# A fused two-layer graph kernel: in its second graph stage the logits joined with the turning, the second normalisation on ScalarE, the neighbour weightings one round later

## The chip, the cores and the metric
The kernel runs on one core of one Trainium2 chip. Its whole computation is one launch. The metric is the device time of that launch in microseconds, a median over runs.

## What is computed
The input is `x` (64 graphs of 256 nodes with 256 features, fp32) and a 0/1 adjacency `adj` (64 x 256 x 256). Two layers follow, each a graph part and a feed-forward part with a residual and a layer normalisation. Layer 0's feed-forward part is an LSTM over the nodes of each graph with a gate, and layer 1's graph part is a normalised graph convolution. The changed stage does the end of the first and all of the second, and the normalisation after it:

```python
lstm_out = _lstm(x, W_ih, W_hh, b_ih, b_hh)
logits = jnp.einsum('bth,lh->btl', lstm_out, W_lin) + b_lin
g = argmax(logits, axis=-1)[..., None]
w = g * lstm_out
inc = jnp.cumsum(w, axis=1)
prefix = inc - w
suffix = inc[:, -1:, :] - inc
x2 = x1 + 2.0 * lstm_out + prefix * fw_att + suffix * bw_att
...
adj = adj + eye(n)
deg_inv_sqrt = adj.sum(axis=-1) ** -0.5
adj_norm = deg_inv_sqrt[:, :, None] * adj * deg_inv_sqrt[:, None, :]
x3 = x2 + adj_norm @ (layernorm(x2) @ W) + b
xn3 = layernorm(x3)
```

`x3` and `xn3` are then used by layer 1's feed-forward part.

## The kernel before
The kernel has five stages, one after the other, with a barrier of blocks between them: the first graph stage, the LSTM, the second graph stage (`stage_gnn1`, L1022), the tropical stage, and the last feed-forward stage. The change touches the second graph stage alone. In the trace it lies between 1552 and about 2156 us.

A graph is a tile of 256 nodes by 256 features, held as 128 partitions by two blocks; `t` counts blocks of nodes (NT = 2) and `k` blocks of features (KD = 2). The work on the graphs is a software pipeline. The helper `rounds` gives every engine the same sequence of rounds, `r` = 0 to 67. In round `r` a section written `if live(lag)` works on graph `r - lag`; the first 8 and the last 6 rounds are written out, those between are a loop of two. Inside a round each engine has its own fixed order of sections, and semaphores join the engines. Semaphore values count graphs: `wait_past(act, wh_ready, n)` waits until `n` graphs have been weighted. The order of each engine in a full round is this (the lag in brackets):

- TensorE: cumulative products `y` from the weightings (2, L1300 to L1305), turning of `x3` (4), products with `W` into `ps_w` (3, L1319), logits (0, L1330) and turning of `h_t` into `ps_h` (0, helper `turn`, L1291), aggregation with `adjt` (3, L1341), turning of `xn3` (4), turning of `xn` (2).
- VectorE: `x2` from `y` and `s` (2, L1391), its statistics (L1369, L1375), `x2b` (L1396), normalisation `xn3` (4, L1380), normalisation `xn` (2, also L1380), logits with bias and `picked` (0, L1413, L1415), four weightings into `whf` and `whb` (0, L1421), `x3` (3, L1433) and its statistics, `is_zero` and `deg_safe` (2), `s` = `x1` + `h2` (0, L1452).
- ScalarE: copy of `x3t` (4), `hs` from `ps_w` scaled by `dinv` (3, L1250), `h2` = 2 `ps_h` (0, L1258), the state of the next graph gathered into `h_t` (-1, L1235), row sums of `adj` (2, L1267), copy of `xn3t` (4), copy of `xn_t` (2).
- GpSimd: `vare` and `rstd` from the statistics of `x2` (2, L1202, L1204), the identity added to `adjt` (2, L1209), `vare3` and `rstd3` (3, L1215, L1217), then `power`, `keep` and `dinv` (2, to L1226).
- SyncE issues the stores of `x3t`, `xn3` and `xn3t` and the loads of `adjt`, `adj` and `x1`, in that mixed order, each behind a wait.

`h2`, `x2`, `x3`, `xn`, `h_t` and each PSUM tile have one buffer; `s`, `whf`, `whb`, `x2b`, the loaded tiles and the three outputs have two. Before the first round TensorE and VectorE wait until all constants have landed (`CONST_DMAS`, 11 of them). In rows of the trace the stage's prefix and the digits are left out of names: `g_x` stands for x1, x2 and x3, `g_xn` for xn and xn3, `g_rstd` for rstd and rstd3, `g_h` for h2, `g_ht` for h_t.

Of the kernel before, what the change touches and what calls it, by code (L numbers as in the profile page):

```python
# [1021 lines left out]
def stage_gnn1(nc, a, hx, x1_dram, x3t_dram, xn3t_dram, xn3_dram):  # L1022
# [3 lines left out]
    with ExitStack() as ctx:  # L1026
# [6 lines left out]
        def sem(name):  # L1033
# [4 lines left out]
        w_lin = sb("g1_wlin", [P, KD, 2])  # L1038
        b_lin = sb("g1_blin", [P, NT, 2])
# [14 lines left out]
        h2 = sb("g1_h2", [P, NT, D])  # L1054
        logit = sb("g1_logit", [P, NT, 2])
# [21 lines left out]
        one = sb("g1_one", [P, NT])  # L1077
# [6 lines left out]
        ps_logit = ps("g1_ps_logit", [P, NT, 2])  # L1084
        ps_h = ps("g1_ps_h", [P, NT, D])
# [13 lines left out]
        h_t_ready, h_done, h2_ready, logit_ready, picked_ready, wh_ready, y_done = (  # L1099
            sem("g1_" + n) for n in ("h_t_ready", "h_done", "h2_ready", "logit_ready", "picked_ready", "wh_ready",  # L1100
# [10 lines left out]
            sem("g1_" + n) for n in ("x3_ready", "stats3_ready", "mv3_ready", "vare3_ready", "rstd3_ready", "xn3_ready"))  # L1111
        x3t_done, x3t_ready, xn3t_done, xn3t_ready = (
            sem("g1_" + n) for n in ("x3t_done", "x3t_ready", "xn3t_done", "xn3t_ready"))
        CONST_DMAS = 11
# [22 lines left out]
        def _(sp):  # L1137
            sp.dma_start(w_lin[:, :, :], a["w_lin_t"].rearrange("(k p) c -> p k c", p=P)).then_inc(const_in, 16)
# [51 lines left out]
        def _(pool):  # L1190
# [3 lines left out]
            pool.wait_ge(consts_set, 3)  # L1194
            pool.wait_ge(const_in, 16 * CONST_DMAS)

            def body(graph, live):
# [33 lines left out]
        def _(act):  # L1231
# [6 lines left out]
            def body(graph, live):  # L1238
# [13 lines left out]
                if live(0):  # L1252
                    n, i, j = graph(0)

                    act.wait_ge(h_done, n + 1)
                    wait_past(act, wh_ready, n)
                    wait_past(act, s_ready, n)
                    act.activation(h2[:, :, :], ps_h[:, :, :], ACT.Copy, scale=2.0).then_inc(h2_ready, 1)  # L1258
# [25 lines left out]
        def _(pe):  # L1284
# [9 lines left out]
            def body(graph, live):  # L1294
# [27 lines left out]
                if live(0):  # L1322
# [37 lines left out]
        def _(dve):  # L1360
            dve.memset(ones_sq[:, :], 1.0).then_inc(ones_set, 1)
            dve.wait_ge(const_in, 16 * CONST_DMAS)
            dve.tensor_scalar(fw[:, :], fw[:, :], 0.5, None, ALU.mult)
# [20 lines left out]
            def body(graph, live):  # L1384
# [1563 lines left out]
```

## Time and profile before

| what | value |
|---|---|
| median of 3 runs | 6029.61 us (6028.96 to 6030.96) |
| the profiled execution | 6013.3 us, its span 6011.5 us |
| TensorE busy | 5471.9 us, 91% |
| VectorE busy | 4967.6 us, 83% |
| ScalarE busy | 3371.2 us, 56% |
| GpSimd busy | 1711.0 us, 28% |
| mean granted TensorE clock | 0.965 |

Busy time is summed per engine, and the engines run beside each other. TensorE's matmul records are pipelined and overlap, so that a busy share near 100% is not the same as work at full rate; the start times of its records tell more. One fp32 product leaves two records in the trace, one turn of a 128x128 block a single one.

### The profile page before, as it was taken

The page shows a single profiled execution, that of the slowest core. Times are in us where ns is not written, and L with a number is a line of the kernel's source. Part 1 is how long each engine was busy: PE and PEld are TensorE (multiplying, and loading weights), DVE is VectorE, ACT ScalarE, POOL GpSimd, SP SyncE. Part 2 cuts the span into 40 slices and gives each one's busy share as a digit, 9 for nine tenths or more (in the row PEclk, how much of TensorE's full clock was granted, in tenths as well). Part 3 has the DMA queues.
Part 4 walks back from the last instruction along what each step waited for, and adds up shares of the span by engine and source line. Part 5 has one row for each costly group of instructions (what it writes and reads, how often), then busy time and mean ns, then how long its engine had stood idle before and what let it go on. Part 6 is the DMA issues. An engine that isn't in the chain of part 4 may idle for free. (4 is left out here: it accounts for less than half of the span.)

```text
span 6011.5 us, 111926 instructions
## 1 busy us (share of the span) xinstructions
PE 5471.9 (91%) x33194; PEld 3624.3 (60%) x33194; DVE 4967.6 (83%) x9615; ACT 3371.2 (56%) x6793; POOL 1711.0 (28%) x3552
## 2 busy tenths in 40 slices
PE   9998999999899969999999985875759999999999
PEld 6666888888788856666666653443434444444444
DVE  8996664444699969999999997986859999999998
ACT  6664444444455546666666651221228787877787
POOL 3331000000255536666666651375530000000000
PEclk9999999999899989999999997987979999999999
DMA  4442001000355522222222211365541212222221
GB/s 136 135 135 69 0 11 50 0 0 0 96 176 176 177 90 73 73 73 73 73 73 72 71 67 32 114 219 179 171 161 66 89 63 85 69 84 83 71 84 49
DMA packets 359806, 529.10 MB, mean 88 GB/s; under 512 B 28256, under 2 KB 298208, under 8 KB 359680
## 3 DMA queue, kind: packets, MB, share of 16 engines
q1 hardware_dynamic: 323376, 401.62, 20.5%
q0 software_dynamic: 36304, 126.13, 6.1%
q8 instruction: 38, 0.62, 0.0%
q14 instruction: 88, 0.72, 0.0%
HBM read 298.52 MB, written 229.14 MB: 88 GB/s over the span
## 5 line engine op out<-in xcount | busy, mean ns | idle before, releaser
L1894 PE MATMUL t_fetched<-t_wpart,t_onehot 128*128 128x512 f32 x4096 | 1222.0, 420 | 35.8 <-DVE t_tout L1999 15.9
L1999 DVE SCALAR_TENSOR_TENSOR t_tout<-t_fetched,t_top,t_tout 128x1024 f32<-128x1024 f32 x896 | 1149.0, 1282 | 36.3 <-PE t_fetched L1894 4.8
L1894 PEld LDWEIGHTS t_fetched<-t_wpart,t_onehot 128*128 128x128 f32 x4096 | 691.8, 188 | 269.2 <-DVE t_tout L1999 131.2
L2832 DVE SCALAR_TENSOR_TENSOR f_line<-f_hinge,f_vec,f_line 128x1024 f32<-128x1024 f32 x512 | 655.2, 1280 | 82.5 <-ACT f_hinge L2710 48.3
L2322 PE MATMUL ts_fetched<-t_wpart,ts_onehot 128*128 128x512 f32 x1608 | 508.7, 451 | 165.2 <-ACT ts_onehot L2297 65.3
L961 PE MATMUL l_ps<-l_wih,l_x 128*64 128x128 f32 (+1 forms) x6144 | 531.6, 308 | 1.0 <-DVE l_ps L597 1.0
L2322 PEld LDWEIGHTS ts_fetched<-t_wpart,ts_onehot 128*128 128x128 f32 x1608 | 305.6, 208 | 316.6 <-DVE ts_tout L2390 202.3
L961 PE MATMUL l_ps<-l_whh,l_ht 128*64 128x128 f32 (+1 forms) x6144 | 492.6, 309 | 0.0
L2762 PE MATMUL f_pso<-f_fused,f_wd 128*128 128x512 f32 x1024 | 461.9, 594 | 23.1 <-DVE f_ox L2828 23.1
L2749 PE MATMUL f_psc<-f_x,f_wc 128*128 128x512 f32 x1024 | 482.8, 594 | 0.0
L925 ACT ACTIVATE l_act<-l_ps 128x128 f32<-128x128 f32 x1024 | 253.9, 276 | 407.0 <-PE l_ps L961 407.0
L2749 PE MATMUL f_psg<-f_x,f_wg 128*128 128x512 f32 x1024 | 481.2, 592 | 0.0
L2294 ACT ACTIVATE ts_dist<-ts_index,t_pminus 128x256 f32<-128x256 f32 (+2 forms) x140 | 79.5, 568 | 653.6 <-PE ts_index L2313 544.5
L961 PEld LDWEIGHTS l_ps<-l_wih,l_x 128*64 128x64 f32 x6144 | 388.7, 137 | 75.4 <-issue 1.8
L2710 ACT ACTIVATE f_hinge<-f_pst,f_vec 128x1024 f32<-128x1024 f32 x384 | 430.8, 1122 | 0.0
L961 PEld LDWEIGHTS l_ps<-l_whh,l_ht 128*64 128x64 f32 x6144 | 372.5, 137 | 80.9 <-DVE l_ht L617 0.2
L2390 DVE SCALAR_TENSOR_TENSOR ts_tout<-ts_fetched,ts_top,ts_tout 128x1024 f32<-128x1024 f32 x296 | 380.0, 1284 | 14.0 <-PE ts_fetched L2322 3.5
L2762 PEld LDWEIGHTS f_pso<-f_fused,f_wd 128*128 128x128 f32 x1024 | 193.2, 190 | 273.5 <-issue 230.6
L2749 PEld LDWEIGHTS f_psg<-f_x,f_wg 128*128 128x128 f32 x1024 | 194.6, 190 | 245.1 <-issue 245.1
L2832 DVE SCALAR_TENSOR_TENSOR f_line<-f_spare,f_vec,f_line 128x1024 f32<-128x1024 f32 x224 | 287.8, 1285 | 44.3 <-DVE f_line L2832 44.3
L1842 ACT ACTIVATE t_tout<-t_fetched,t_top 128x1024 f32<-128x1024 f32 x128 | 142.9, 1117 | 322.8 <-PE t_fetched L1894 322.8
L2719 ACT ACTIVATE f_spare<-f_pst,f_vec 128x1024 f32 x224 | 241.2, 1138 | 137.2 <-DVE f_pause L2857 136.8
(384 smaller groups left out, 10720.8 us busy)
## 6 DMA issues: line engine op xcount, KB each, us to landing
t<-t_tout SPq DMA_DIRECT2D x128, 512.0 KB, 2.6
f_t<-t SPq DMA_DIRECT2D x64, 1024.0 KB, 5.3
g_adj<-in_adj SPq DMA_DIRECT2D x128, 256.0 KB, 3.0
g_adjt<-in_adjt SPq DMA_DIRECT2D x128, 256.0 KB, 2.7
t_x<-x_normalised SPq DMA_DIRECT2D x130, 128.0 KB, 2.3
g_x<-in_x SPq DMA_DIRECT2D x64, 256.0 KB, 2.8
x_kept<-g_x SPq DMA_DIRECT2D x64, 256.0 KB, 2.1
g_x<-x_kept SPq DMA_DIRECT2D x64, 256.0 KB, 2.8
```

Of the source, the lines that this page charges most:

```text
L925: act.activation(act_g[q][:, :], gate(j, q), function).then_inc(act_ready[q], 1)
L961: mm = pe.matmul(out[:, :, 0:P] if n > 1 else ps_g[j][c2 * HB:(c2 + 1) * HB, q * LANE:q * LANE + P], source[:, k, :], w[:, k, q:q + n, c2, ...
L1842: act.activation(t_out[j][:, :], fetched[0][:, :], ACT.Identity, bias=top[j][:, 0, 0:1]).then_inc(first_ready, 1)
L1894: mm = pe.matmul(fetched[c % RING][:, h * CH:(h + 1) * CH], one_hot[g][:, c % GRP * P:(c % GRP + 1) * P], w_part[part][:, k, h * CH:(h + 1 ...
L1999: dve.scalar_tensor_tensor(t_out[j][:, :], column[:, :], value, t_out[j][:, :], ALU.add, ALU.max)\
L2322: mm = pe.matmul(fetched[buf][:, h * CH:(h + 1) * CH], one_hot[b][:, at * P:(at + 1) * P], w_part[part][:, half, h * CH:(h + 1) * CH], sta ...
L2390: dve.scalar_tensor_tensor(t_out[j][:, :], column[:, :], top[j][:, c:c + 1], (t_out if c else t_in)[j][:, :], ALU.add, ALU.max).then_inc(f ...
L2710: act.activation(hinge[v][:, k, :], ps_t[:, :], ACT.Relu, bias=column(u, "knot", k))\
L2719: act.activation(spare[:, ds(k, 1), :].rearrange("p o t -> p (o t)"), ps_t[:, :], ACT.Relu, bias=column(u, "knot", k + SURE))
L2749: mm = pe.matmul(ps_[:, :], w_[:, k, u * P:(u + 1) * P], x[j][:, k, h * HB:(h + 1) * HB], start=(k == 0), stop=(k == KD - 1))
L2762: mm = pe.matmul(ps_o[k][:, h * HB:(h + 1) * HB], w_d[:, u, k * P:(k + 1) * P], fused[u % 2][:, h * HB:(h + 1) * HB], start=(u == 0), stop ...
L2832: dve.scalar_tensor_tensor(acc[:, :], source, column(u, "bend", k), acc[:, :], ALU.mult, ALU.add)\
```

## The change
In TensorE's part, the separate logit products and the turning of `h_t` become one product per block: `h_t` is the stationary operand and `turn_lin`, the identity with the two columns of `W_lin` beside it (130 columns), is the moving one. `ps_h` therefore gets a layout of its own with two banks, and holds one pair of partial logits for each `k`. `h2` copies turned state and logits together, 520 columns instead of 512. VectorE adds the two partial logits and twice the bias from `h2` (two small additions instead of one) and picks. This and the weightings move from lag 0 to lag 1 and, within the round, from behind `xn` to behind `x2b`. The second normalisation moves from VectorE to ScalarE, two operations of 128x256 (`Identity` with a scale and a bias per row) behind the copy of `h2`; for it GpSimd computes `minus_mean3` and `shift3` in addition. `s` now waits for `h2` itself. Two more constants are loaded.

```diff
-            sp.dma_start(w_lin[:, :, :], a["w_lin_t"].rearrange("(k p) c -> p k c", p=P)).then_inc(const_in, 16)
+            sp.dma_start(turn_lin[:, :, P:P + 2], a["w_lin_t"].rearrange("(k p) c -> p k c", p=P)).then_inc(const_in, 16)
+            for k in range(KD):
+                sp.dma_start(turn_lin[:, k, 0:P], a["ident"]).then_inc(const_in, 16)
...
                     pool.wait_ge(mv3_ready, n + 1)
+                    wait_past(pool, xn3_ready, n)
+                    pool.tensor_tensor(minus_mean3[:, :], mv3[:, :, 0], minus_one[:, :], ALU.mult)
                     pool.tensor_tensor(vare3[:, :], mv3[:, :, 1], eps[:, :], ALU.add).then_inc(vare3_ready, 1)
                     pool.wait_ge(vare3_ready, n + 1)
                     pool.tensor_tensor(rstd3[:, :], vare3[:, :], half[:, :], ALU.pow).then_inc(rstd3_ready, 1)
+                    pool.wait_ge(rstd3_ready, n + 1)
+                    pool.tensor_tensor(shift3[:, :], minus_mean3[:, :], rstd3[:, :], ALU.mult).then_inc(shift3_ready, 1)
...
                     act.wait_ge(h_done, n + 1)
                     wait_past(act, wh_ready, n)
                     wait_past(act, s_ready, n)
-                    act.activation(h2[:, :, :], ps_h[:, :, :], ACT.Copy, scale=2.0).then_inc(h2_ready, 1)
+                    act.activation(h2[:, :, :, :], ps_h[:, :, :, 0:P + 2], ACT.Copy, scale=2.0).then_inc(h2_ready, 1)
+                if live(4):
+                    n, i, j = graph(4)
+
+                    act.wait_ge(shift3_ready, n + 1)
+                    wait_past(act, x3t_stored[j], 48 * i)
+                    for t in range(NT):
+                        last = act.activation(xn3_out[j][:, t, :], x3[:, t, :], ACT.Identity, scale=rstd3[:, t:t + 1],
+                                              bias=shift3[:, t:t + 1])
+                    last.then_inc(xn3_ready, 1)
                 if live(-1):
                     turned_h(graph(-1)[0])
...
                     pe.wait_ge(h_t_ready, n + 1)
                     wait_past(pe, h2_ready, n)
-                    wait_past(pe, logit_ready, n)
                     for t in range(NT):
                         for k in range(KD):
-                            pe.matmul(ps_logit[:, t, :], h_t[:, k, t * P:(t + 1) * P], w_lin[:, k, :],
-                                      start=(k == 0), stop=(k == KD - 1))
-                    turn(ps_h, h_t).then_inc(h_done, 1)
+                            last = pe.matmul(ps_h[:, t, k, 0:P + 2], h_t[:, k, t * P:(t + 1) * P], turn_lin[:, k, :],
+                                             start=True, stop=True)
+                    last.then_inc(h_done, 1)
...
                     dve.tensor_tensor(x2b[j][:, :, :], x2[:, :, :], b_all[:, :, :], ALU.add).then_inc(x2b_ready, 1)
-                if live(4):
-                    n, i, j = graph(4)
-
-                    dve.wait_ge(rstd3_ready, n + 1)
-                    wait_past(dve, x3t_stored[j], 48 * i)
-                    normalised(n, xn3_out[j], x3, mv3, rstd3, xn3_ready)
+                if live(1):
+                    n, i, j = graph(1)
+
+                    dve.wait_ge(h2_ready, n + 1)
+                    dve.tensor_tensor(half_logit[:, :, :], h2[:, :, 0, P:P + 2], two_b[:, :, :], ALU.add)\
+                       .then_inc(half_logit_ready, 1)
+                    dve.wait_ge(half_logit_ready, n + 1)
+                    dve.tensor_tensor(logit[:, :, :], h2[:, :, 1, P:P + 2], half_logit[:, :, :], ALU.add).then_inc(logit_ready, 1)
+                    dve.wait_ge(logit_ready, n + 1)
+                    dve.tensor_tensor(picked[:, :], logit[:, :, 1], logit[:, :, 0], ALU.is_gt).then_inc(picked_ready, 1)
+                    dve.wait_ge(picked_ready, n + 1)
+                    wait_past(dve, y_done, n - 1)
+                    for wh, att in ((whf, fw), (whb, bw)):
+                        for t in range(NT):
+                            last = dve.scalar_tensor_tensor(wh[j][:, t, :].rearrange("p (k u) -> p k u", k=KD), h2[:, t, :, 0:P],
+                                                            picked[:, t:t + 1], att[:, :].rearrange("p (k u) -> p k u", k=KD),
+                                                            ALU.mult, ALU.mult)
+                    last.then_inc(wh_ready, 1)
                 if live(2):
                     n, i, j = graph(2)
 
                     dve.wait_ge(rstd_ready, n + 1)
                     wait_past(dve, xt_done, n)
                     normalised(n, xn, x2, mv, rstd, xn_ready)
-                if live(0):
-                    n, i, j = graph(0)
-
-                    dve.wait_ge(h_done, n + 1)
-                    dve.tensor_tensor(logit[:, :, :], ps_logit[:, :, :], b_lin[:, :, :], ALU.add).then_inc(logit_ready, 1)
...
-                    dve.wait_ge(h2_ready, n + 1)
-                    wait_past(dve, y_done, n - 1)
-                    for wh, att in ((whf, fw), (whb, bw)):
...
                 if live(0):
                     n, i, j = graph(0)
 
+                    dve.wait_ge(h2_ready, n + 1)
                     dve.wait_ge(x1_loaded[j], 16 * i + 16)
                     wait_past(dve, x2_ready, n - 1)
-                    dve.tensor_tensor(s[j][:, :, :], x1_in[j][:, :, :], h2[:, :, :], ALU.add).then_inc(s_ready, 1)
+                    dve.tensor_tensor(s[j][:, :, :].rearrange("p t (k u) -> p t k u", k=KD),
+                                       x1_in[j][:, :, :].rearrange("p t (k u) -> p t k u", k=KD), h2[:, :, :, 0:P], ALU.add).then_inc(s_ready, 1)
```

## Rows read from the trace of the kernel before

**Rows 1.** Windows: us, busy us by engine (x instructions), PEclk, DMA share, GB/s.
```profile
1800.00:1900.00 100.00, 99.59 (x586) 87.96 (x585) 94.23 (x304) 54.36 (x123) 51.17 (x104) 1.00 0.56 175
```
**Rows 2.** Waits, 1600 to 2129 us: who, for whom, us in total, times, longest.
```profile
DVE g_xn L1380 <- POOL g_rstd L1204: 15.3, 59, 0.3
PEld g_ps_agg L1341 <- ACT g_hs L1250: 14.8, 59, 0.3
```
**Rows 3.** Timeline of VectorE (start us, length us): x2 in rounds 4 and 64.
```profile
1594.81 0.68 DVE L1391 TENSOR_TENSOR g_x<-g_ps_y,g_s 128x512 f32<-128x512 f32 x1
...
2129.93 0.68 DVE L1391 TENSOR_TENSOR g_x<-g_ps_y,g_s 128x512 f32<-128x512 f32 x1
```
**Rows 4.** Timeline of TensorE, one steady round: logits and the turn of h.
```profile
1854.59 0.95 PE L1330 MATMUL g_ps_logit<-g_wlin,g_ht 128*128 128x2 f32 x8
...
1855.40 0.63 PE L1291 MATMUL g_ps_h<-g_ident,g_ht 128*128 128x128 f32 x4
```
**Rows 5.** Timeline of TensorE, same round: turn of xn3, last products of y.
```profile
1857.72 0.58 PEld L1291 LDWEIGHTS g_ps_xn3t<-g_ident,g_xn 128*128 128x128 f32 x4
...
1857.93 0.60 PE L1291 MATMUL g_ps_xn3t<-g_ident,g_xn 128*128 128x128 f32 x4
...
1860.97 0.59 PE L1305 MATMUL g_ps_y<-g_whb,g_after 128*128 128x256 f32 x2
```
**Rows 6.** Timeline of VectorE, same round.
```profile
1853.45 0.68 DVE L1391 TENSOR_TENSOR g_x<-g_ps_y,g_s 128x512 f32<-128x512 f32 x1
...
1855.70 0.73 DVE L1380 TENSOR_SCALAR g_xn<-g_x,g_mv,g_rstd 128x256 f32<-128x256 f32 x2
...
1856.68 1.00 DVE L1380 TENSOR_SCALAR g_xn<-g_x,g_mv,g_rstd 128x256 f32<-128x256 f32 x2 [0.26 <-POOL g_rstd L1204]
...
1857.61 0.15 DVE L1413 TENSOR_TENSOR g_logit<-g_ps_logit,g_blin 128x4 f32<-128x4 f32 x1
...
1857.98 0.88 DVE L1421 SCALAR_TENSOR_TENSOR g_whf<-g_h,g_picked,g_fw 128x256 f32<-128x256 f32 x2
...
1858.78 0.88 DVE L1421 SCALAR_TENSOR_TENSOR g_whb<-g_h,g_picked,g_bw 128x256 f32<-128x256 f32 x2
...
1859.57 0.87 DVE L1433 SCALAR_TENSOR_TENSOR g_x<-g_ps_agg,g_dinv,g_x2b 128x256 f32<-128x256 f32 x2
...
1862.34 0.69 DVE L1391 TENSOR_TENSOR g_x<-g_ps_y,g_s 128x512 f32<-128x512 f32 x1
```
**Rows 7.** Timeline, a late round: hs on ScalarE and the aggregation's weight loads.
```profile
2147.37 0.84 ACT L1250 ACTIVATE g_hs<-g_ps_w,g_dinv 128x256 f32<-128x256 f32 x2 [1.91 <-POOL g_dinv L1226]
2148.26 0.73 PEld L1341 LDWEIGHTS g_ps_agg<-g_hs,g_adjt 128*128 128x128 f32 x4 [1.86 <-ACT g_hs L1250]
```
**Rows 8.** Timeline of ScalarE, steady round: h2, h_t, first of the adj copies.
```profile
1856.07 0.60 ACT L1258 ACTIVATE g_h<-g_ps_h 128x512 f32<-128x512 f32 x1
...
1856.57 1.09 ACT L1235 ACTIVATE g_ht<-hx 128x512 f32 x1
...
1857.57 0.40 ACT L1267 ACTIVATE g_adj<-g_adj 128x256 f32<-128x256 f32 x1
```
**Rows 9.** Timeline of GpSimd, steady round.
```profile
1856.61 0.92 POOL L1209 TENSOR_TENSOR g_adjt<-g_adjt,g_ident 128x128 f32<-128x128 f32 x2
...
1861.60 0.20 POOL L1215 TENSOR_TENSOR g_vare<-g_mv,g_eps 128x2 f32<-128x2 f32 x1 [4.07 <-DVE g_mv L1375]
...
1863.85 0.20 POOL L1226 TENSOR_TENSOR g_dinv<-g_power,g_keep 128x2 f32<-128x2 f32 x1
```
**Rows 10.** Timeline, start of the stage: a constant's issue, the first logits.
```profile
1553.24 0.46 SPq L1139 DMA_DIRECT2D g_ident<-in_ident  x1
...
1563.86 1.87 PE L1330 MATMUL g_ps_logit<-g_wlin,g_ht 128*128 128x2 f32 x8 [14.69 <-DMA g_w<-in_W]
```
**Rows 11.** Windows, a stretch of the tropical stage.
```profile
3750.00:3800.00 50.00, 41.28 (x171) 24.62 (x168) 47.60 (x66) 11.45 (x18) 12.52 (x26) 1.00 0.22 78
```
**Rows 12.** Groups of ScalarE's instructions by line: one of four table loads.
```profile
L1588 ACT ACT_TABLE_LOAD x1 | 1.3, 1283 | 2.8 <-DVE t_scale L1643 2.8
```

More of the change, by code:

```diff
@@ L1037, in stage_gnn1 @@
         w = sb("g1_w", [P, KD, D])
-        w_lin = sb("g1_wlin", [P, KD, 2])
-        b_lin = sb("g1_blin", [P, NT, 2])
+        turn_lin = sb("g1_turnlin", [P, KD, P + 2])
+        b_lin, two_b = sb("g1_blin", [P, NT, 2]), sb("g1_twob", [P, NT, 2])
         ones_sq = sb("g1_ones_sq", [P, P])
@@ L1053, in stage_gnn1 @@
         h_t = sb("g1_ht", [P, KD, N])
-        h2 = sb("g1_h2", [P, NT, D])
-        logit = sb("g1_logit", [P, NT, 2])
+        h2 = sb("g1_h2", [P, NT, KD, P + 2])
+        half_logit, logit = sb("g1_halflogit", [P, NT, 2]), sb("g1_logit", [P, NT, 2])
         picked = sb("g1_picked", [P, NT])
@@ L1076, in stage_gnn1 @@
         eps = sb("g1_eps", [P, NT])
-        one = sb("g1_one", [P, NT])
+        one, minus_one = sb("g1_one", [P, NT]), sb("g1_minusone", [P, NT])
+        minus_mean3, shift3 = sb("g1_minusmean3", [P, NT]), sb("g1_shift3", [P, NT])
         row_sum = sb("g1_row_sum", [P, NT])
@@ L1083, in stage_gnn1 @@
         dinv = [sb(f"g1_dinv{j}", [P, NT]) for j in range(2)]
-        ps_logit = ps("g1_ps_logit", [P, NT, 2])
-        ps_h = ps("g1_ps_h", [P, NT, D])
+        ps_h = ps("g1_ps_h", [P, NT, KD, 2 * P])
         ps_y = ps("g1_ps_y", [P, NT, D])
@@ L1098, in stage_gnn1 @@
         x3t_stored = [sem(f"g1_x3t_stored{j}") for j in range(2)]
-        h_t_ready, h_done, h2_ready, logit_ready, picked_ready, wh_ready, y_done = (
-            sem("g1_" + n) for n in ("h_t_ready", "h_done", "h2_ready", "logit_ready", "picked_ready", "wh_ready",
+        h_t_ready, h_done, h2_ready, half_logit_ready, logit_ready, picked_ready, wh_ready, y_done = (
+            sem("g1_" + n) for n in ("h_t_ready", "h_done", "h2_ready", "half_logit_ready", "logit_ready", "picked_ready", "wh_ready",
                                      "y_done"))
@@ L1111, in stage_gnn1 @@
             sem("g1_" + n) for n in ("x3_ready", "stats3_ready", "mv3_ready", "vare3_ready", "rstd3_ready", "xn3_ready"))
+        shift3_ready = sem("g1_shift3_ready")
         x3t_done, x3t_ready, xn3t_done, xn3t_ready = (
             sem("g1_" + n) for n in ("x3t_done", "x3t_ready", "xn3t_done", "xn3t_ready"))
-        CONST_DMAS = 11
+        CONST_DMAS = 13
         LAST = 4
@@ L1193, in _ @@
             pool.memset(one[:, :], 1.0).then_inc(consts_set, 1)
-            pool.wait_ge(consts_set, 3)
+            pool.memset(minus_one[:, :], -1.0).then_inc(consts_set, 1)
+            pool.wait_ge(consts_set, 4)
             pool.wait_ge(const_in, 16 * CONST_DMAS)
@@ L1362, in _ @@
             dve.wait_ge(const_in, 16 * CONST_DMAS)
+            dve.tensor_scalar(two_b[:, :, :], b_lin[:, :, :], 2.0, None, ALU.mult)
             dve.tensor_scalar(fw[:, :], fw[:, :], 0.5, None, ALU.mult)
@@ L1408, in body @@
                     normalised(n, xn, x2, mv, rstd, xn_ready)
-                if live(0):
-                    n, i, j = graph(0)
-                    dve.wait_ge(h_done, n + 1)
-                    dve.tensor_tensor(logit[:, :, :], ps_logit[:, :, :], b_lin[:, :, :], ALU.add).then_inc(logit_ready, 1)
-                    dve.wait_ge(logit_ready, n + 1)
-                    dve.tensor_tensor(picked[:, :], logit[:, :, 1], logit[:, :, 0], ALU.is_gt).then_inc(picked_ready, 1)
-                    dve.wait_ge(picked_ready, n + 1)
-                    dve.wait_ge(h2_ready, n + 1)
-                    wait_past(dve, y_done, n - 1)
-                    for wh, att in ((whf, fw), (whb, bw)):
-                        for t in range(NT):
-                            last = dve.scalar_tensor_tensor(wh[j][:, t, :], h2[:, t, :], picked[:, t:t + 1], att[:, :],
-                                                            ALU.mult, ALU.mult)
-                    last.then_inc(wh_ready, 1)
                 if live(3):
```

## The prediction

> **What bounds the stage now.** The change touches one stage, the second graph stage. I read the windows first, to see how full each engine is; then who waited for whom, for what ends the idle time; then one steady round in order of time, because a stage in which three engines are nearly full is set by a loop of waits and not by a share. In the 100 us window TensorE is busy 99.6 us and VectorE 94.2, ScalarE and GpSimd about half [rows 1]. The waits in 59 rounds are small: VectorE waited 15.3 us for GpSimd's `rstd`, TensorE's weight loads 14.8 us for `hs` [rows 2]. VectorE waits for nothing else, and GpSimd's `rstd` comes from VectorE's own statistics, so VectorE with that short trip closes the loop that sets the round. From the start of `x2` in round 4 to its start in round 64 there are 60 rounds: 2129.93 - 1594.81 = 535.1 us, 8.92 us each [rows 3]. TensorE's own work is 8.92 less 14.8/59 = 0.25 of waiting, 8.67 us: almost level, but behind.
>
> **TensorE's part.** From the first turn of `xn3` at 1857.93 to the last pair of `y` at 1860.97 lie 8 turn records of 128 columns and 10 of `y` of 256, in 3.04 us [rows 5]; if the pitch goes by columns that is 28 times 0.109, so a turn takes 0.109 and a record of `y` 0.217. The logits start at 1854.59 and the turning of `h` at 1855.40, 0.81 us, and its four turns are 0.44 [rows 4]: 1.25 us go. In come 4 products of 130 columns, two records each: 8 x 0.11 = 0.87 us. TensorE saves 0.38 and has 8.29 us of work. The bounds are the pitch of the logits' records, 0.81 for eight, and that of 256 columns, 1.74, which would be 0.5 worse than today. It lies between `w` products and aggregation, and, as the loop below shows, in TensorE's slack, so I price it at nothing; the cover is over 1 us.
>
> **VectorE's part.** Out goes the second normalisation, 0.73 us (at 1855.70 in [rows 6]). In comes one small addition; `logit` to the first weighting is 1857.98 - 1857.61 = 0.37 for two such operations, so three are 0.55. The four weightings have the same shape; their source now has gaps, priced at nothing for lack of a row. The wait of 0.26 for `rstd` goes, since the weightings now cover it. VectorE's own work falls to about 8.92 - 0.26 - 0.73 + 0.18 = 8.11 us. What counts is the order: the weightings (of the graph before) now stand directly behind `x2b`, ahead of `xn` and `x3`.
>
> **ScalarE's part, and the new loop.** `h2` has one buffer. Its copy already waits for `wh_ready`; that used to mean weightings of the round before and now means those of this round. Behind the copy, in ScalarE's queue, stands the second normalisation. TensorE turns its result before it turns `xn` and before it starts `y` of the next round, and VectorE's `x2` waits for `y`. So one loop goes once round all three engines in every round, from the end of the weightings to the end of the next:
> - a hand-over from engine to engine: 0.05, as from `hs` (2147.37 + 0.84) to the aggregation at 2148.26 [rows 7]; there are three, 0.15.
> - copy of `h2`: the next operation starts 1856.57 - 1856.07 = 0.50 later [rows 8]. (520 columns instead of 512 add 0.01.)
> - second normalisation: two operations of 128x256 with a per-row scale, as `hs`: 0.84 [rows 7].
> - TensorE, turn of `xn3`, turn of `xn`, six products of `y`: from 1857.93 to 1860.97 + 0.59 = 1861.56, 3.63, and 0.07 for the first weight load after an idle gap (between nothing and the 0.21 from load at 1857.72 to product): 3.70 [rows 5].
> - `x2`, statistics, `x2b`: 1855.70 - 1853.45 = 2.25 [rows 6].
> - three small operations, 0.55; weightings 1857.98 to 1858.78 + 0.88 = 1859.66, 1.68 [rows 6]: 2.23.
> Sum: 0.15 + 0.50 + 0.84 + 3.70 + 2.25 + 2.23 = **9.67 us** a round, against 8.92. It binds in the rounds that have both an `h2` and an `xn3`, 4 to 63, which closes 60 intervals: 60 x 9.67 - 535.1 = 45 us more.
>
> Is everything else ready in time? Count from the end of the weightings. ScalarE releases `xn3` at 1.39; `xn` (1.00 at most) is done before that. `y` ends at 5.15. VectorE could be at `x2` by 1.44 + 2.77 = 4.21 (start of `x3` to the next `x2`, 1862.34 - 1859.57 in [rows 6]), so it stands idle for 1 us. TensorE goes on with the turn of `x3`, 0.44, and the `w` products, 8 x 0.217: 7.3. GpSimd's `dinv`: today from `vare3` at 1861.60 to 1863.85 + 0.20 it takes 2.45 [rows 9]; the two new small operations (`minus_mean3` ahead, `shift3` behind the power) add some 0.27 each, so about 3.0; starting near 3.4 (`x3` from 1.44, and 1861.60 - 1859.57 = 2.03 more) it ends near 6.4, before the `w` products. `hs` ends near 8.2, the aggregation near 10.05, and `xn3` of the next round comes at 9.67 + 1.39 = 11.06. So TensorE waits about 1.0 us there each round and its saving is lost in that wait. SyncE's loads of `adjt`, `adj` and `x1` now stand behind a later store of `xn3`; they are issued one to two rounds (10 to 19 us) ahead of their use and cost nothing.
>
> **Unknown costs.** GpSimd's addition to `adjt` (0.92) now falls beside the weightings instead of `xn`. Beside it, `xn` takes 1.00 instead of the 0.73 of `xn3` [rows 6, 9], so another operation might lose up to 0.27; I take nothing, because `x2` at 1862.34 with GpSimd at work beside it takes 0.69 and no row but `xn` shows a loss, and keep 0.27, 16 us, for the range. The Trainium skill (SBUF — State Buffer, Who interferes with whom) says that a VectorE instruction with two SBUF inputs contends with a GpSimd instruction that reads SBUF, which is the case of the weightings beside this addition; by it the sum would be nearer 9.9 us a round, and 61 us in all. Hand-overs: 0 to 0.10 each, -9 to +9 us. The normalisation reads SBUF and not PSUM; the `adj` copy of that shape takes 0.40 [rows 8], a little under half of the 0.84, so down to -4 us.
> Outside the steady rounds: two more constant loads at 0.46 of issue each [rows 10], +1; the first two logit-and-turn groups run before TensorE's clock has risen, 1.87 for the logits' records against 0.95 later [rows 4, 10], and there the joined ones take about twice 0.87 instead of 1.87 and twice 0.44, -2; in rounds 2 and 3 `xn` waits for the weightings, +1 to +2; at the end `shift3` and a slightly longer normalisation, +1. Together +2, between -3 and +5.
>
> The profiled execution took 6013.3 us (span 6011.5), 16 below the median of the three runs; 45 + 2 = 47 gives 6060 on its scale and 6029.6 + 47 = **6077 us** on that of the median. About 0.2%, 12 us, is what a measurement of this kernel can tell from no change.
>
> **Rivals.**
> *Other loops set the round (faster).* If `y` were done before VectorE gets to `x2`, the round would go by VectorE's `x3`, which waits for `xn3` to leave its single buffer: 0.05 + 1.34 + 0.05 + 2.77 + 2.25 + 2.23 = 8.69 us, 14 us less, so 6018. For it: VectorE and TensorE both lose work. Against: from the weightings' end to `y`'s end there are 5.15 us where 4.4 would be break-even, and every piece of them has a row. Chance 0.08, nearly all for a wait that I misread.
> *Gains and losses cancel*: 0.04.
> *The loop, and contention or clock on top (more than 6095).* Weightings with the full 0.27, hand-overs at 0.10: 10.1 us, 6102. TensorE's granted clock is 1.00 here; busy 8.29 of 9.67, 86%, it could fall. A stretch of the tropical stage at 83% busy has 1.00 [rows 11], which speaks against it. At a mean of 0.9 the 3.70 would be 4.1, +25 us. Chance 0.15.
> *A table load before each Identity.* ScalarE's load is 1.28 us [rows 12], one on the loop each round would be +77, 6154. The tropical stage alternates Identity at L1842 and Copy at L1836 without loads between; 0.02.
> *The loop as summed*: 0.71. It ends on the slow side, as do the last two. Faster 0.08, same 0.04, slower 0.88. The range, 6052 to 6104, takes in the loop with all its bounds and leaves out the first, the second and the fourth rival.
>
> **What would show it.** In the after profile: steady rounds of 9.67; VectorE waits some 0.95 us a round in `x2` for `y`, a new first row in its waits; TensorE waits about 1 us a round for ScalarE's `xn3` at the turn; ScalarE waits for the weightings before the `h2` copy; joined products 0.87 a round; `rstd` wait gone; clock still 1.00. Wrong if `x2` never waits for `y`, or rounds are below 8.9 us.

## The result, and the profile after

The changed kernel takes 6118.02 us (median of 4 runs, 6114.24 to 6120.51), the kernel before 6030.28 beside it: a ratio of 1.0145, 95% interval 1.0129 to 1.0161. It is 88 us slower. The forecast was 6077, 47 us slower, with 6104 as the upper end. The direction and the loop hold, the size does not.

The window of the changed kernel that answers to [rows 1] (the same columns: us, busy us of TensorE, its weight loads, VectorE, ScalarE and GpSimd, granted clock, DMA share, GB/s):

```profile
1800.00:1900.00 100.00, 83.55 (x461) 70.94 (x460) 77.95 (x249) 56.54 (x128) 45.88 (x104) 1.00 0.48 150
```

TensorE has fallen from 99.6 to 83.6 us of 100 and VectorE from 94.2 to 78.0, at a granted clock of 1.00. No engine is full: the stage is set by waits. The waits in 51 rounds (who, for whom, us in total, times, longest):

```profile
ACT g_h L1266 <- issue: 100.6, 51, 2.0
PEld g_ps_xn3t L1308 <- ACT g_xn L1273: 99.9, 51, 2.0
...
DVE g_x L1447 <- ACT g_xn L1273: 58.5, 51, 1.1
DVE g_x L1408 <- PE g_ps_y L1322: 37.3, 51, 0.9
...
PEld g_ps_agg L1357 <- ACT g_hs L1258: 14.7, 51, 0.3
```

Per round ScalarE waits 2.0 us ahead of its copy of `h2`, TensorE's weight loads 2.0 for `xn3`, VectorE 1.15 at `x3` (L1447) for `xn3` and 0.73 at `x2` (L1408) for `y`. VectorE's wait for `rstd` of [rows 2] is gone; that for `hs` is as it was. The starts of `x2` in rounds 4 and 64, as in [rows 3]:

```profile
1598.13 0.69 DVE L1408 TENSOR_TENSOR g_x<-g_ps_y,g_s 128x512 f32<-128x512 f32 x1 [0.48 <-PE g_ps_y L1322]
...
2221.52 0.69 DVE L1408 TENSOR_TENSOR g_x<-g_ps_y,g_s 128x512 f32<-128x512 f32 x1 [0.81 <-PE g_ps_y L1322]
```

That is 623.4 us, 10.39 a round instead of 8.92, and 88.3 us more: nearly the whole difference lies in these 60 rounds. From its first DMA issue to the first of the next stage, the stage takes 700.2 us (1555.83 to 2256.01) instead of 609.1 (1552.80 to 2161.88), so some 3 us lie outside them. One of them in order of time, from `x2` to the next `x2` (start us, length us, engine, line; to be read beside [rows 5, 6, 8]):

```profile
1857.85 0.69 DVE L1408 TENSOR_TENSOR g_x<-g_ps_y,g_s 128x512 f32<-128x512 f32 x1 [0.65 <-PE g_ps_y L1322]
...
1860.11 0.15 DVE L1418 TENSOR_TENSOR g_halflogit<-g_h,g_twob 128x4 f32<-128x4 f32 x1
...
1860.69 1.08 DVE L1428 SCALAR_TENSOR_TENSOR g_whf<-g_h,g_picked,g_fw 128x256 f32<-128x256 f32 x2
...
1860.99 1.11 POOL L1213 TENSOR_TENSOR g_adjt<-g_adjt,g_ident 128x128 f32<-128x128 f32 x2
1861.70 1.07 DVE L1428 SCALAR_TENSOR_TENSOR g_whb<-g_h,g_picked,g_bw 128x256 f32<-128x256 f32 x2
1862.69 0.72 DVE L1397 TENSOR_SCALAR g_xn<-g_x,g_mv,g_rstd 128x256 f32<-128x256 f32 x2
1862.85 0.60 ACT L1266 ACTIVATE g_h<-g_ps_h 128x520 f32<-128x520 f32 x1 [1.93 <-issue]
1863.36 1.08 ACT L1273 ACTIVATE g_xn<-g_x,g_shift,g_rstd 128x256 f32<-128x256 f32 x2
...
1864.48 0.42 PEld L1308 LDWEIGHTS g_ps_xn3t<-g_ident,g_xn 128*128 128x128 f32 x4 [1.92 <-ACT g_xn L1273]
...
1864.57 0.88 DVE L1447 SCALAR_TENSOR_TENSOR g_x<-g_ps_agg,g_dinv,g_x2b 128x256 f32<-128x256 f32 x2 [1.15 <-ACT g_xn L1273]
...
1867.58 0.59 PE L1322 MATMUL g_ps_y<-g_whb,g_after 128*128 128x256 f32 x2
...
1868.30 0.69 DVE L1408 TENSOR_TENSOR g_x<-g_ps_y,g_s 128x512 f32<-128x512 f32 x1 [0.81 <-PE g_ps_y L1322]
```

The forecast loop stands in these lines. The weightings end at 1861.70 + 1.07 = 1862.77, the copy of `h2` starts at 1862.85, the normalisation behind it ends at 1864.44, TensorE's turn starts at 1864.48, `y` ends at 1867.58 + 0.59 = 1868.17, and `x2` starts at 1868.30. `x3` (1864.57) has stood waiting since `xn` ended, because ScalarE's normalisation was still reading the one buffer of `x3`.

### The profile page after: what moved, and what is told of

It reads as the page before. It is cut to its first block and busy times, and to the rows that moved or that the text cites. A ratio compares the mean times of both kernels' runs of the same rounds, so it can differ in the third digit from the quotient of the medians.

```text
span 6118.6 us, 111674 instructions
## 1 busy us (share of the span) xinstructions
PE 5472.0 (89%) x32938; PEld 3609.2 (59%) x32938; DVE 4951.9 (81%) x9552; ACT 3427.6 (56%) x6921; POOL 1738.7 (28%) x3681
```

## The experiments

A round in this table is the mean from `x2` of round 4 to `x2` of round 64 in the one profiled execution. Times are compared through the ratio to the kernel before on the same chip.

| kernel | us | before | ratio (95%) | us a round |
|---|---|---|---|---|
| e1 normalisation ahead of h2 | 6020.7 | 6017.8 | 1.0006 (0.9996 to 1.0016) | 9.02 |
| e2 two buffers of h2 | 6022.9 | 6017.8 | 1.0009 (0.9999 to 1.0019) | 9.02 |
| e3 normalisation on VectorE | 6057.8 | 6017.8 | 1.0066 (1.0048 to 1.0084) | 9.62 |
| e4 weightings in their old place | 6052.0 | 6017.4 | 1.0058 (1.0041 to 1.0074) | 9.58 |
| e5 GpSimd's addition later | 6078.0 | 6017.8 | 1.0102 (1.0084 to 1.0120) | 9.99 |
| e6 = e1 + e5 | 5997.1 | 6017.4 | 0.9966 (0.9954 to 0.9978) | 8.65 |
| e7 = e6, y ahead of the turns | 6058.0 | 6017.4 | 1.0068 (1.0051 to 1.0085) | 9.60 |
| e8 scale without bias | 6093.0 | 6017.4 | 1.013, one run | 10.21 |
| e9 joined products alone | 6034.7 | 6028.0 | 1.0012 (1.0002 to 1.0021) | 9.14 |
| e10 = e6, turn of xn3 as cover | 6006.4 | 6028.0 | 0.9964 (0.9951 to 0.9978) | 8.62 |
| e11 the changed kernel again | 6115.4 | 6028.0 | 1.0144 (1.0128 to 1.0159) | 10.39 |
| e12 = e10, xn ahead of weightings | 6023.4 | 6016.1 | 1.0012 (1.0003 to 1.0021) | 9.06 |

The diffs are against the changed kernel where nothing else is said. e11 is that kernel itself:

> The changed kernel once more, beside the kernel before on the same chip as the other two: 10.39 us a round against 8.92, 88 us, a ratio of 1.0145 as first measured, give or take 0.001.

It repeats the result in a second measurement: 1.0144 (1.0128 to 1.0159) and 10.39 us a round.

**Is it this loop?** e1 swaps two sections on ScalarE:

```diff
                     last.then_inc(hs_ready, 1)
+                if live(4):
...
+                    act.wait_ge(shift3_ready, n + 1)
...
+                    last.then_inc(xn3_ready, 1)
                 if live(0):
...
                     act.activation(h2[:, :, :, :], ps_h[:, :, :, 0:P + 2], ACT.Copy, scale=2.0).then_inc(h2_ready, 1)
-                if live(4):
...
-                    act.wait_ge(shift3_ready, n + 1)
...
-                    last.then_inc(xn3_ready, 1)
```

> The changed kernel with one order swapped: on ScalarE the second normalisation stands ahead of the copy of h2, and so no longer waits for the weightings. Theory (one loop: weightings, h2 copy, normalisation, turn of xn3, y, x2, weightings; 10.39 us a round measured): the loop is open, VectorE is left as the bound with 10.39 less its two waits of 1.15 and 0.73, some 8.45 us a round. 60 x (8.45 - 10.39) = -116, about 6002 us; the waits of x3 for xn3 and of x2 for y go to nearly nothing. Rival (the single h2 buffer itself, whose copy waits for the weightings, holds the round up through h_t, the row sums or the joined products): rounds stay above 10 us and the time above 6090.

e2 opens the same link in another way:

```diff
-        h2 = sb("g1_h2", [P, NT, KD, P + 2])
+        h2 = [sb(f"g1_h2{j}", [P, NT, KD, P + 2]) for j in range(2)]
...
-                    wait_past(act, wh_ready, n)
-                    wait_past(act, s_ready, n)
+                    wait_past(act, wh_ready, n - 1)
+                    wait_past(act, s_ready, n - 1)
```

> The changed kernel with two buffers of h2, so that its copy waits for the weightings of the round before; the order on ScalarE is left as changed. Theory of the one loop: opened at the same link as in the swap of order, so the same 8.4 to 8.5 us a round, 5998 to 6005 us. Rival (the cost lies in the moved normalisation being slow on ScalarE or in TensorE's queue, and not in the h2 wait): little or no gain, above 6090.

Both take the round from 10.39 to the same 9.02, and the waits for `xn3`, at the turn and at `x3`, disappear. So the loss comes from the loop through the `h2` wait and the normalisation behind it: an order swap that removes no work gives nearly all of it back. But 8.45 was expected. The timeline of e1 shows what is late next:

```profile
1853.62 1.07 DVE L1428 SCALAR_TENSOR_TENSOR g_whb<-g_h,g_picked,g_bw 128x256 f32<-128x256 f32 x2
...
1854.62 0.73 DVE L1397 TENSOR_SCALAR g_xn<-g_x,g_mv,g_rstd 128x256 f32<-128x256 f32 x2
...
1855.40 0.66 PE L1308 MATMUL g_ps_t<-g_ident,g_xn 128*128 128x128 f32 x4 [0.16 <-DVE g_xn L1397]
...
1855.89 0.60 PE L1317 MATMUL g_ps_y<-g_whf,g_before 128*128 128x256 f32 x2
...
1858.05 0.59 PE L1322 MATMUL g_ps_y<-g_whb,g_after 128*128 128x256 f32 x2
...
1858.68 0.69 DVE L1408 TENSOR_TENSOR g_x<-g_ps_y,g_s 128x512 f32<-128x512 f32 x1 [0.32 <-PE g_ps_y L1322]
```

`xn`, now behind the weightings, ends at 1855.35; its turn follows at 1855.40, `y` behind it from 1855.89 to 1858.05 + 0.59 = 1858.64, and `x2` at 1858.68. A second loop, through weightings, `xn`, its turn and `y`, closes at 8.91 us in the rounds written out. It was hidden under the first. Its pieces, from one such round of e1 (`x2` at 1597.08), are 2.26 from `x2` to the small operations, 0.58 for these, 2.00 to the start of `xn`, 0.78 to its turn, 0.50 to `y`, 2.75 for `y` and 0.04 to `x2`: 8.91.

**The normalisation back on VectorE.** e3 removes it from ScalarE, and `minus_mean3` and `shift3` from GpSimd:

```diff
-                    pool.tensor_tensor(minus_mean3[:, :], mv3[:, :, 0], minus_one[:, :], ALU.mult)
...
-                    pool.wait_ge(rstd3_ready, n + 1)
-                    pool.tensor_tensor(shift3[:, :], minus_mean3[:, :], rstd3[:, :], ALU.mult).then_inc(shift3_ready, 1)
...
                     dve.tensor_tensor(x2b[j][:, :, :], x2[:, :, :], b_all[:, :, :], ALU.add).then_inc(x2b_ready, 1)
+                if live(4):
...
+                    dve.wait_ge(rstd3_ready, n + 1)
+                    wait_past(dve, x3t_stored[j], 48 * i)
+                    normalised(n, xn3_out[j], x3, mv3, rstd3, xn3_ready)
                 if live(1):
```

> The changed kernel with the second normalisation back on VectorE, behind x2b and ahead of the weightings, and without minus_mean3 and shift3 on GpSimd; joined products and later weightings stay. Theory of the one loop: open as well, since TensorE's turn of xn3 no longer hangs on ScalarE behind h2. VectorE then carries 8.45 + 0.73 = 9.2 us a round: 60 x (9.2 - 10.39) = -71, about 6047, slower than before by 17. Rival (the later weightings are at fault by themselves): above 6090.

The first loop is open here too, but 9.62 is above the 9.2 expected. The second loop accounts for it, because the normalisation now stands ahead of the weightings in it:

```profile
1599.12 0.73 DVE L1384 TENSOR_SCALAR g_xn<-g_x,g_mv,g_rstd 128x256 f32<-128x256 f32 x2
1599.77 0.15 DVE L1411 TENSOR_TENSOR g_halflogit<-g_h,g_twob 128x4 f32<-128x4 f32 x1
```

The next operation starts 0.65 after it, and from there to the start of `xn` it is 2.53 us instead of e1's 2.58. In the rounds written out that gives 8.91 + 0.65 - 0.05 = 9.51, and they take 9.50; 9.62 is the mean with the rounds inside the loop.

**Why the weightings took longer.** In the changed kernel a pair takes 1.08 us instead of 0.88 [rows 6]. Gaps in their source or GpSimd beside them could be the cause. The changed kernel's own first round answers half of it, where GpSimd has nothing to do yet:

```profile
1572.05 0.88 DVE L1428 SCALAR_TENSOR_TENSOR g_whf<-g_h,g_picked,g_fw 128x256 f32<-128x256 f32 x2
1572.85 0.88 DVE L1428 SCALAR_TENSOR_TENSOR g_whb<-g_h,g_picked,g_bw 128x256 f32<-128x256 f32 x2
```

The same gapped source costs 0.88 there, so the gaps are not the cause. e5 moves GpSimd's addition:

```diff
                     pool.wait_ge(adjt_loaded[j], 16 * i + 16)
+                    pool.wait_ge(xn_ready, n + 1)
```

> The changed kernel, in which GpSimd's addition to adjt waits for xn of this round, so that it runs behind the weightings and not beside them. It only adds a wait. Theory of contention: the weightings go back from 1.08 a pair with a long first one to 0.88 a pair, the loop from 10.39 to about 10.0, -24 us, about 6094. Rival (the gaps in the weightings' source and destination make them long): the pair stays at 1.08 and the time at 6118 or above.

The pair goes back, and the round falls by 0.40 to 9.99. The groups over 300 us (mean ns of one), first e5, then the changed kernel with the normalisation in its first line:

```profile
L1429 DVE SCALAR_TENSOR_TENSOR g_whf<-g_h,g_picked,g_fw 128x256 f32<-128x256 f32 x60 | 26.4, 483 | 1.1
```

```profile
L1273 ACT ACTIVATE g_xn<-g_x,g_shift,g_rstd 128x256 f32<-128x256 f32 x58 | 31.3, 588 | 0.0
...
L1428 DVE SCALAR_TENSOR_TENSOR g_whf<-g_h,g_picked,g_fw 128x256 f32<-128x256 f32 x58 | 31.4, 583 | 1.0
```

The mean of one is 483 against 583 ns. The changed kernel's line of the weightings, over one round (least, median and longest of one in ns), shows how that is spread:

```profile
L1428 DVE SCALAR_TENSOR_TENSOR g_whf<-g_h,g_picked,g_fw x2: 487/585/683, 1860.7 to 1861.1; 128x256 f32<-128x256 f32 x2
L1428 DVE SCALAR_TENSOR_TENSOR g_whb<-g_h,g_picked,g_bw x2: 474/574/673, 1861.7 to 1862.3; 128x256 f32<-128x256 f32 x2
```

In each pair one takes its plain time and one 0.2 us more: two of the four run longer beside the addition, 0.40 us in all. The Trainium skill (SBUF — State Buffer, Who interferes with whom) says that a VectorE instruction with two SBUF inputs contends with a GpSimd instruction that reads SBUF; these runs agree.

**What makes the normalisation long on ScalarE.** It takes 588 ns an operation, not the 471 of `hs`. e8 leaves out the subtraction of the mean, so its `xn3` is other data:

```diff
-                        last = act.activation(xn3_out[j][:, t, :], x3[:, t, :], ACT.Identity, scale=rstd3[:, t:t + 1],
-                                              bias=shift3[:, t:t + 1])
+                        last = act.activation(xn3_out[j][:, t, :], x3[:, t, :], ACT.Copy, scale=rstd3[:, t:t + 1])
```

> The changed kernel with ScalarE's second normalisation as Copy with the per-row scale alone: the subtraction of the mean is left out, so xn3 is other data. It asks what makes an operation take 0.588 us where hs takes 0.472. Theory: the per-row bias is the surplus, so it falls to about 0.41 to 0.47 and rounds by 0.15 to 0.25 us. Rival (reading and writing SBUF beside the weightings, or the second operand of scale, is the surplus): it stays near 0.59.

```profile
L1273 ACT ACTIVATE g_xn<-g_x,g_rstd 128x256 f32<-128x256 f32 x58 | 25.9, 497 | 0.0
```

e8 changes two things, the per-row bias and the function (`Identity` to `Copy`), and together they are worth 91 ns an operation; two operations account for the round's fall from 10.39 to 10.21. A line of the kernel before tells the two apart. It is the tropical stage's `Exp` on the same shape, with the same two per-row operands:

```profile
L1829 ACT ACTIVATE t_allowed<-t_restlow,t_shiftr,t_scale 128x256 f32<-128x256 f32 x128 | 75.0, 586 | 0.0
```

It takes 586 ns with another function, so the surplus goes with the operands. This line was there to price the moved normalisation before the change. The 26 ns between `hs` (471) and e8 (497) remain; `hs` reads PSUM and the normalisation SBUF, but no run tries that alone.

**The parts alone.** e4 puts logits and weightings back behind `xn`, one round earlier:

```diff
-                if live(1):
-                    n, i, j = graph(1)
+                if live(2):
...
+                    normalised(n, xn, x2, mv, rstd, xn_ready)
+                if live(0):
+                    n, i, j = graph(0)
...
                     last.then_inc(wh_ready, 1)
-                if live(2):
...
-                    normalised(n, xn, x2, mv, rstd, xn_ready)
```

e9 has the edits of e3 and of e4 together, so that only the joined products are left of the change; against the kernel before:

```diff
-                            pe.matmul(ps_logit[:, t, :], h_t[:, k, t * P:(t + 1) * P], w_lin[:, k, :],
-                                      start=(k == 0), stop=(k == KD - 1))
-                    turn(ps_h, h_t).then_inc(h_done, 1)
+                            last = pe.matmul(ps_h[:, t, k, 0:P + 2], h_t[:, k, t * P:(t + 1) * P], turn_lin[:, k, :],
+                                             start=True, stop=True)
+                    last.then_inc(h_done, 1)
```

> The changed kernel with logits and weightings back at lag 0 behind xn; joined products and the second normalisation on ScalarE stay. Theory: the long loop is open, but VectorE has nothing left to lay over GpSimd's rstd: in the kernel before the wait was 0.26 with the normalisation of xn3 (0.73) ahead of it, so it becomes about 1.0, and the 0.73 saved is spent in it. With one more small operation (0.18) rounds take about 9.1 us, some 11 us above the kernel before. Rival (moving the normalisation off VectorE frees it): 8.4 us a round, 30 us below.

> The kernel before with one part of the change: logits joined with the turning and read from h2, both as changed; normalisation and weightings stay where they were. Theory: TensorE is not the bound, so its 0.38 us a round buy nothing, and the one small operation more on VectorE, which is, costs 0.18: 60 x 0.18 = 11, between 0.1% and 0.3% slower than before. Rival (TensorE's pace counts): faster than before by up to 20 us.

e9 came out as expected, 0.12% slower: TensorE's saving buys nothing alone. Its 9.14 us a round come from the slowest of its ten executions (6040.4 us) and would make 13 us, while the medians lie 7 apart. e4 is slower than expected, and its timeline tells why:

```profile
1851.80 0.20 POOL L1220 TENSOR_TENSOR g_minusmean<-g_mv,g_minusone 128x2 f32<-128x2 f32 x1 [4.34 <-DVE g_mv L1392]
...
1854.12 0.15 DVE L1392 BATCH_NORM_AGGREGATE g_mv<-g_stats 128x2 f32<-128x6 f32 x1
...
1854.97 0.20 POOL L1234 TENSOR_TENSOR g_dinv<-g_power,g_keep 128x2 f32<-128x2 f32 x1
1855.12 0.20 POOL L1206 TENSOR_TENSOR g_vare<-g_mv,g_eps 128x2 f32<-128x2 f32 x1
...
1855.40 0.69 POOL L1208 TENSOR_TENSOR g_rstd<-g_vare,g_half 128x2 f32<-128x2 f32 x1
...
1856.12 1.00 DVE L1397 TENSOR_SCALAR g_xn<-g_x,g_mv,g_rstd 128x256 f32<-128x256 f32 x2 [1.28 <-POOL g_rstd L1208]
```

The same of e9, GpSimd alone:

```profile
1850.81 0.19 POOL L1219 TENSOR_TENSOR g_vare<-g_mv,g_eps 128x2 f32<-128x2 f32 x1 [4.26 <-DVE g_mv L1379]
...
1853.07 0.20 POOL L1230 TENSOR_TENSOR g_dinv<-g_power,g_keep 128x2 f32<-128x2 f32 x1
1853.42 0.55 POOL L1206 TENSOR_TENSOR g_vare<-g_mv,g_eps 128x2 f32<-128x2 f32 x1 [0.16 <-DVE g_mv L1379]
```

In e4 GpSimd takes 3.17 us from its first operation behind the statistics of `x3` (1851.80) to `dinv` (1854.97), with `minus_mean3` and `shift3` among them; in e9 it takes 2.26. So it is still on the way to `dinv` when the statistics of `x2` are there (1854.27) and takes up `vare` at 1855.12 only, and `xn` waits 1.28 us for `rstd`, where 1.0 was expected (in the mean of 55 rounds 1.37). The 0.73 that VectorE has lost to ScalarE was the cover of this wait, and more than that came back as waiting.

**Better orders.** e6 joins e1 and e5:

> The order swap of e1 and the later addition of e5 together. e1 showed a second loop at 8.9 us: weightings, xn behind them on VectorE, its turn on TensorE, y of the next round behind that turn, x2. Theory: this loop has the weightings in it too, so taking GpSimd's addition away from beside them shortens it by 0.4, to about 8.5 us a round, 24 us below e1, about 5997 on the chip of e1. Rival (after e1 something outside the weightings holds, such as TensorE's own work with its wait for hs): no better than 8.8 us, above 6012.

It takes 8.65 us a round, with a ratio of 0.9966 (0.9954 to 0.9978), and beats both kernels. Three attempts to go on followed. e7 is e6 with `y` placed behind the aggregation, ahead of both turns, and the turn of `xn` ahead of that of `xn3`; on TensorE, against e6:

```diff
-                if live(2):
-                    n, i, j = graph(2)
-
-                    pe.wait_ge(wh_ready, n + 1)
...
                     last.then_inc(agg_done, 1)
+                if live(1):
+                    n, i, j = graph(1)
+
+                    pe.wait_ge(wh_ready, n + 1)
...
                     turn(ps_t, xn).then_inc(xt_done, 1)
+                if live(4):
...
+                    turn(ps_xn3t, xn3_out[j]).then_inc(xn3t_done, 1)
```

> e6 with TensorE's y products of the graph just weighted placed behind the aggregation of the same round, ahead of the turns of xn and of xn3. Theory: neither turn lies between weightings and y any more; VectorE's work of 8.1 and TensorE's 8.29 plus its wait of 0.25 for hs remain, about 8.55 us a round, so as e6 or up to 5 us less, 5992 to 5997. If e6 stays at 8.8 or above because of the turn of xn, this one is clearly below it.

The round rises to 9.60 us. Its waits show two new ones, `x3` for the aggregation and the products with `W` for the copy of `xn_t`, which in ScalarE's queue stands behind that of `xn3t`:

```profile
DVE g_x L1448 <- PE g_ps_agg L1347: 72.7, 47, 1.7
PEld g_ps_w L1326 <- ACT g_xnt L1296: 46.9, 48, 1.0
```

ScalarE's and TensorE's lines show where the second comes from:

```profile
1862.57 0.60 ACT L1292 ACTIVATE g_xn3t<-g_ps_xn3t 128x512 f32<-128x512 f32 x1 [2.31 <-PE g_ps_xn3t L1309]
...
1863.71 0.30 PEld L1326 LDWEIGHTS g_ps_w<-g_w,g_xnt 128*128 128x128 f32 x2 [0.98 <-ACT g_xnt L1296]
```

The turn of `xn3` is now the last of TensorE's round. ScalarE copies it first and `xn_t` only after it, and TensorE's products with `W` wait 0.98 us for that. With the wait for `hs` (0.29) the 9.60 leave 8.33 of TensorE's own work, about the 8.29 of the forecast: TensorE's order and ScalarE's queue close a loop of their own, and `x3` waits as a consequence. This is read from the rows; no run takes that wait away.

e10 takes the turn of `xn3` ahead of the aggregation, and to have it ready there, the normalisation ahead of `hs` on ScalarE; against e6:

```diff
+                if live(4):
...
+                    last.then_inc(xn3_ready, 1)
                 if live(3):
...
                     last.then_inc(hs_ready, 1)
...
+                if live(4):
...
+                    turn(ps_xn3t, xn3_out[j]).then_inc(xn3t_done, 1)
                 if live(3):
...
                     last.then_inc(agg_done, 1)
```

> Changed kernel with GpSimd's addition later (e5), ScalarE's normalisation ahead of both hs and the h2 copy, and TensorE's turn of xn3 ahead of the aggregation. Theory of loops: e6 is held at 8.52 us in unlooped rounds by weightings, xn, both turns, y, x2 and by TensorE's work with its wait for hs of 0.27. Taking the turn of xn3 (0.44) out from between xn and y shortens the first to 8.1, and the same turn now covers the wait for hs, which leaves TensorE's own 8.3. So 8.3 in unlooped and some 8.45 on average against 8.65 of e6: 12 to 15 us below e6, 30 to 36 us below before. Rival (ScalarE's longer way to hs, or GpSimd's shift3, delays the aggregation): no better than e6.

It gains nothing clear over e6 (0.9964 against 0.9966; 8.50 against 8.62 in the first rounds written out, 8.62 against 8.65 in the mean), which corrects my reading of e6's loop. e10's timeline:

```profile
1856.92 0.60 PE L1309 MATMUL g_ps_xn3t<-g_ident,g_xn 128*128 128x128 f32 x4
...
1858.58 0.73 DVE L1398 TENSOR_SCALAR g_xn<-g_x,g_mv,g_rstd 128x256 f32<-128x256 f32 x2
...
1859.37 0.66 PE L1309 MATMUL g_ps_t<-g_ident,g_xn 128*128 128x128 f32 x4
...
1859.86 0.60 PE L1318 MATMUL g_ps_y<-g_whf,g_before 128*128 128x256 f32 x2
...
1862.65 0.69 DVE L1409 TENSOR_TENSOR g_x<-g_ps_y,g_s 128x512 f32<-128x512 f32 x1 [0.31 <-PE g_ps_y L1323]
```

`xn` starts at 1858.58 and its turn at 1859.37, after a wait for it (23.6 us in 50 rounds, 0.47 each). In e6 TensorE filled that wait with the turn of `xn3` (0.44), so it lengthened the loop by 0.1 us at most; the expectation counted it there in full. e12 is e10 with `xn` between `picked` and the weightings, and GpSimd's addition behind the weightings:

```diff
                     dve.tensor_tensor(picked[:, :], logit[:, :, 1], logit[:, :, 0], ALU.is_gt).then_inc(picked_ready, 1)
+                if live(2):
...
+                    normalised(n, xn, x2, mv, rstd, xn_ready)
+                if live(1):
...
                     dve.wait_ge(picked_ready, n + 1)
...
-                    pool.wait_ge(xn_ready, n + 1)
+                    if live(1):
+                        pool.wait_ge(wh_ready, graph(1)[0] + 1)
```

> The kernel of e10 with xn on VectorE between picked and the weightings, and GpSimd's addition waiting for the weightings in place of xn. e10 taught that its 8.50 us are a loop in which the turn of xn3 has no part: xn 0.79 with the hand-over, turn of xn 0.49, y 2.75, hand-over 0.04, x2 to the first small operation 2.26, small operations 0.58, weightings 1.59. Theory: the weightings, now last, feed y directly, so xn and its turn leave the loop except for the 0.73 that xn takes on VectorE and 0.2 to 0.3 of its wait for rstd, which only x2b and the small operations (1.16 of 1.4) cover now: 0.05 + 2.75 + 0.04 + 2.26 + 0.58 + 0.25 + 0.73 + 1.59 = 8.25, below TensorE's own 8.3. So 8.3 to 8.4 in unlooped rounds and 8.4 to 8.5 on average against 8.62: 7 to 13 us below e10, a ratio to the kernel before of 0.994 to 0.995. Rival (the turns of xn, not the weightings, still hold y back, or the loop's branch gives the gain back): equal to e10, 0.9964.

It is slower, 9.06 us. VectorE now waits at `is_zero` for the row sums:

```profile
1855.46 0.87 DVE L1439 SCALAR_TENSOR_TENSOR g_whb<-g_h,g_picked,g_bw 128x256 f32<-128x256 f32 x2
...
1856.42 0.60 ACT L1277 ACTIVATE g_h<-g_ps_h 128x520 f32<-128x520 f32 x1 [2.73 <-issue]
...
1856.92 1.09 ACT L1245 ACTIVATE g_ht<-hx 128x512 f32 x1
...
1858.31 0.41 ACT L1286 ACTIVATE g_adj<-g_adj 128x256 f32<-128x256 f32 x1
...
1858.84 0.17 DVE L1462 TENSOR_SCALAR g_is_zero<-g_row_sum 128x2 f32<-128x2 f32 x1 [0.64 <-ACT g_adj L1286]
```

The weightings end later (1856.33), the copy of `h2` waits for them, and behind it in ScalarE's queue come `h_t` and the row sums, for which `is_zero` waits until 1858.84. That is a third loop through the same wait of the `h2` copy, now by way of `row_sum`. It closes at the round measured: in the round of these lines 5.51 us from `x2` (1850.82) to the end of the weightings, 2.51 to `is_zero`, and 1.07 to the next `x2` (1859.91), 9.09 in all.

## Why the prediction was right and wrong

- **What bounded before, and that the change opens a loop through three engines**: right. The waits at `x2` for `y`, at the turn for `xn3` and ahead of the `h2` copy are there, the wait for `rstd` is gone, the clock is 1.00, and e1 and e2 remove the loss at the link named.
- **Joined products**: right. They cost nothing on the loop, and in e9, where they stand alone, their saving gains nothing.
- **The sum of the loop, 9.67 us**: this is the step that failed, by two terms. For the *weightings* I took 1.68 and an allowance of nothing for GpSimd, with 0.27 as a bound; they measure 2.08 (1860.69 to 1862.77), so 0.40 more. The row of `xn` beside the addition was read as the loss of a whole group, where two of the four weightings lose 0.2 each. The reason for taking nothing was that `x2` keeps its 0.69 beside GpSimd; but `x2` reads one of its inputs from PSUM, the weightings both from SBUF, so its row was not one for their case. For the *second normalisation* I took the 0.84 of `hs`; it measures 1.08, 0.24 more: 0.18 for the per-row bias that `hs` does not have (e8), and about 0.05 left open. I had named a bound only downwards, from the `adj` copy, and none upwards, though the tropical stage's line of 586 ns gives the price. Copy and small operations add 0.04. 9.67 + 0.40 + 0.24 + 0.04 = 10.35, which is the round as it runs where it is written out; in the loop of two every other round takes 10.44, mean 10.39. TensorE's 3.70 (3.69), `x2` to `x2b` at 2.25 (2.26) and the plain hand-overs were right.
- **60 such rounds, and +2 outside them**: the 60 are right. (10.39 - 8.92) x 60 = 88, and the stage as a whole is 91 longer in the traces, so some 3 lie outside, near the 2 of the forecast.
- **Idle time**: for VectorE 0.95 to 1.0 us was forecast, all of it at `x2`; it is 1.9, and the larger part is at `x3`. The forecast's own count has `x3` start at 1.44 and `xn` done by 1.00, so a wait there was in it but not named. For TensorE at the turn of `xn3` about 1.0 was forecast; it is 2.0.
- **The range, and the rival of contention or clock on top (over 6095, chance 0.15)**: this rival is what happened, by its contention and without its clock, which stayed at 1.00. Its 10.1 us, the full 0.27 and dearer hand-overs, were still too few: the unpriced bias and the 0.40 led beyond the range.
- **Rival of the other loops (8.7 us)**: it did not happen, and its size would have been wrong as well. Behind the first loop lies one of 8.91 through `xn` and its turn (e1), which I had not listed.
- **Table loads**: none were added.

## What to carry to other kernels

When a step is moved, first look for what waits on its result in the same round, what stands behind that waiter in its queue, and whether this comes back to the moved step; sum that loop before counting what each engine saves. An operation that leaves the full engine may have been the cover of a wait. And a price per operation is that of the same operands: a per-row bias, or a second engine reading SBUF beside it, has to be bounded upwards too.

## What was not expected of the hardware

- On ScalarE, an operation of 128x256 fp32 from SBUF: 0.40 us with no per-row operand (the `adj` copy, which also sums the rows [rows 8]), 0.497 with a per-row scale (e8), 0.588 with per-row scale and bias.
- Weightings of 128x256 with both inputs in SBUF: 0.48 us alone and 0.68 beside GpSimd's addition; they were unchanged by a step of 130 instead of 128 between the halves of their source.
- Inside the loop of two rounds every second round is longer: by 0.09 us in the changed kernel (10.35 and 10.44 in turn), but by about 0.26 in e1 (8.91 and 9.15 to 9.21). In a long round of e1 0.09 of it lies between the end of `y` and `x2`, and 0.17 on TensorE between the turn of `xn` and the end of `y`. That the loop's branches cause it is inferred from where it occurs; no run tries it.
